# Turning x by halves into four banks, and a feature order that lets W_lat load in runs of 1024 bytes

## The reference

```
k = x @ W_lat + b_lat                        # (2, 512, 128), one for all heads; keys and values
q = x @ W_d + b_d                            # 16 heads of 128
att = softmax(causal(q k^T / sqrt(128)));  y = att @ k
x1 = layernorm(x + y @ W_proj + b_proj)
scores = x1 . router_weight + router_bias;   top 256 of 512 rows of each batch
rows picked: x1 += (gelu(x1 @ w1 + b1) @ w2 + b2) * sigmoid(score)
out = layernorm(x1)
```

## Time and profile before

| | us |
|---|---|
| median of 3 runs | 280.67 |
| lowest and highest | 280.57, 280.73 |
| the profiled execution | 280.85 |
| its span, first to last instruction | 279.1 |
| TensorE matmuls busy | 271.7 (97%) |
| VectorE, ScalarE, GpSimd busy | 218.8, 212.3, 154.2 |
| share of the 16 DMA engines taken by SyncE's queue | 16.4% |

### The profile page before, as it was taken

One profiled execution on the slowest core, in us unless ns is written; L12 is line 12 of the kernel. 1 busy time (PEld: TensorE's weight loads), 2 busy tenths in 40 slices (PEclk: granted clock), 3 DMA queues, 4 the chain that ended last, 5 costly groups with the idle time before them and its releaser, 6 DMA issues.

```text
span 279.1 us, 6206 instructions
## 1 busy us (share of the span) xinstructions
PE 271.7 (97%) x1885; PEld 247.0 (89%) x1885; DVE 218.8 (78%) x701; ACT 212.3 (76%) x578; POOL 154.2 (55%) x214
## 2 busy tenths in 40 slices
PE   8999999999999999999999999999999999999991
PEld 4878999999999998999999999999999999999990
DVE  2698777777777777788789888899988887779882
ACT  3689877777787778887787877787777778879471
POOL 5458444444433336555666866665657847238652
PEclk9999999999999999999999999999999999999997
DMA  5594110111101111111111111110112200020151
GB/s 178 144 293 124 39 40 28 30 36 38 34 25 35 38 39 38 40 38 42 38 38 40 38 40 38 39 37 22 38 39 79 78 21 21 1 76 2 58 171 38
DMA packets 18842, 15.53 MB, mean 56 GB/s; under 512 B 1641, under 2 KB 18178, under 8 KB 18818
## 3 DMA queue, kind: packets, MB, share of 16 engines
q1 hardware_dynamic: 18242, 13.65, 16.4%
q0 software_dynamic: 576, 1.58, 1.6%
HBM read 12.60 MB, written 2.63 MB: 55 GB/s over the span
## 4 chain that ended last, share of the span: by engine, by line
PE 97%; DVE 0%; POOLq 0%; issue 0%; ACT 0%; DVEq 0%
PE bank L412 21%; PE bank L414 20%; PE bank L413 20%; PE bank L547 9%; PE ps_out L412 7%; PE ps_out L413 6%; PE ps_out L414 6%; PE bank L527 3%; PE bank L637 3%; PE bank L470 1%; PE bank L424 1%; POOLq L60 0%; PE bank L676 0%; PE bank L678 0%; PE bank L557 0%
## 5 line engine op out<-in xcount | busy, mean ns | idle before, releaser
L841 ACT ACTIVATE probs<-probs,negmax 128x512 f32<-128x512 f32 (+3 forms) x128 | 72.6, 575 | 6.0 <-DVE negmax L1026 4.6
L1384 POOL TENSOR_TENSOR wd_hi<-wd_raw,zero 128x256 fp32r<-128x256 f32 x31 | 23.8, 768 | 87.5 <-DVE probs L1098 84.5
L849 ACT CAST pT_hi<-bank 128x512 fp32r<-128x512 f32 (+2 forms) x96 | 43.4, 488 | 27.7 <-PE bank L547 27.3
L1026 DVE CUSTOM_DVE_ANT_0 probs<-bank,mask_row 128x512 f32<-128x512 f32 (+3 forms) x128 | 59.2, 482 | 0.7 <-PE bank L504 0.7
L1035 DVE TENSOR_TENSOR pT_lo<-bank,pT_hi 128x512 fp32r<-128x512 f32 (+2 forms) x96 | 52.8, 552 | 6.0 <-ACT pT_hi L849 5.6
L547 PEld LDWEIGHTS bank<-ident_r,prob_words 128*128 128x128 f32 x310 | 33.0, 140 | 5.5 <-ACT probs L893 0.4
L412 PE MATMUL ps_out<-wp_hi,yT_hi 128*128 128x256 f32 x124 | 37.0, 299 | 0.0
L412 PE MATMUL bank<-kT_hi,qT_hi 128*128 128x256 f32 (+2 forms) x94 | 36.5, 388 | 0.0
L413 PE MATMUL ps_out<-wp_lo,yT_hi 128*128 128x256 f32 x124 | 35.0, 282 | 0.0
L414 PE MATMUL ps_out<-wp_hi,yT_lo 128*128 128x256 f32 x124 | 34.9, 282 | 0.0
L1055 DVE TENSOR_TENSOR yT_lo<-bank,yT_hi 128x512 fp32r<-128x512 f32 x31 | 21.4, 690 | 15.9 <-PE bank L414 14.1
(11 more groups left out here) (203 smaller groups left out, 732.1 us busy)
## 6 DMA issues: line engine op xcount, KB each, us to landing
wd_raw<-in_L_attn_W_d SPq DMA_DIRECT2D x32, 128.0 KB, 2.2
wp_raw<-in_L_attn_W_proj SPq DMA_DIRECT2D x32, 128.0 KB, 2.1
wf_raw<-in_L_ffn_w SPq DMA_DIRECT2D x2, 1024.0 KB, 6.7
x_nat<-in_L_attn_x SPq DMA_DIRECT2D x4, 256.0 KB, 3.4
out<-z_all SPq DMA_DIRECT2D x4, 256.0 KB, 2.3
picked<-ranked SPq DMA_DIRECT2D x2, 258.0 KB, 2.7
wlat_raw<-in_L_attn_W_lat SPq DMA_DIRECT2D x1, 128.0 KB, 3.8
bproj_all<-in_L_attn_b_proj SPq DMA_DIRECT2D x1, 128.0 KB, 3.4
```

What stands on the lines that cost most here:

```text
L841: act.activation(p_tile(s, j), p_tile(s, j), ACT.Exp, bias=negmax[:, s, j:j + 1], scale=-1.0, accum_out=sums[:, s, j:j + 1]).then_inc(exp_ ...
L849: act.copy(pT_hi[:, dst], src).then_inc(pt_hi_done, 1)
L1026: dve.tensor_tensor_reduce(p_tile(s, j), score_bank[j], mask_row[:, (TILES - 1 - j) * P:], -SCALE, -MASKED, ALU.add, ALU.min, accum_out=ne ...
L1384: pool.tensor_tensor(hi, src, nothing, ALU.add).then_inc(hi_done, 1)
```

## The change

- A chunk c holds the features c, c + 2, c + 4, ...: W_lat and W_d are loaded with the row 2 p + c on partition p, chunk c. So a partition's part of W_lat is two neighbouring rows, 1024 bytes in one run; of W_d a head's columns are still pieces of 512 bytes. The transposes of x read every second column of the rows as their stationary operand.
- The first batch's x is turned into four banks: half 0 into the first 256 columns of `ps_t0` and `ps_t1`, half 1 into those of `ps_s2` and `ps_s10`. ScalarE copies and VectorE subtracts each of the four by itself, 256 columns each; the semaphores count four steps for the first batch. The second batch is turned as before, apart from the columns read.
- An idle matmul of 256 columns stands between the two halves, and the two of 512 behind them become one of 512 and one of 256.
- VectorE does the two subtractions of half 0 ahead of the rounding of W_lat. The bias turning goes to `ps_s3`, and stands ahead of the last product for kT, whose terms are in another order.

```diff
+        x_banks = [[ps_t0[:, 0:KEEP], ps_t1[:, 0:KEEP]], [ps_s2[:, 0:KEEP], ps_s10[:, 0:KEEP]]]
+        def x_half(t, half, c):
+            return t[:, c, half * KEEP:(half + 1) * KEEP]
-        WAKING, AWAKE = 6, 2
+        WAKING, BETWEEN, AWAKE = 6, (2,), (4, 2)
-            wd = W_d.rearrange("(c p) n -> p c n", p=P)
+            wd = W_d.rearrange("(p c) n -> p c n", p=P)
-            sp.dma_start(wlat_raw[:], W_lat.rearrange("(c p) l -> p c l", p=P)).then_inc(wlat_in, 16)
+            sp.dma_start(wlat_raw[:], W_lat.rearrange("(p c) l -> p c l", p=P)).then_inc(wlat_in, 16)
                     for c in range(CH):
-                        dst = (ps_t0, ps_t1)[c]
+                        dst = (ps_t0, ps_t1)[c][:, half * KEEP:(half + 1) * KEEP] if b else x_banks[half][c]
                         if b and half == 0:
                             pe.wait_ge(x_split, c + 1)
-                        for j in range(2 * half, 2 * half + 2):
+                        for j in range(2):
                             last = pe.transpose(dst[:, j * P:(j + 1) * P].bitcast(F32R),
-                                                x_words[:, b * TILES + j, c * P:(c + 1) * P], ident_r[:, :])
-                        if half:
+                                                x_words[:, b * TILES + 2 * half + j, c:DIM:CH], ident_r[:, :])
+                        if half or not b:
                             last.then_inc(x_turned, 1)
+                    if not b and half == 0:
+                        keep_awake(BETWEEN)
 
             def project_k_first():
                 w_hi, w_lo, x_hi, x_lo = wlat_hi, wlat_lo, xT_hi[0], xT_lo[0]
+                def term(w, x, c, first=False, last=False):
+                    return pe.matmul(ps_kT, w[:, c, :], x[:, c, :], start=first, stop=last, skip_group_check=True)
                 pe.wait_ge(wlat_hi_done, 1)
-                pe.wait_ge(x_hi_done, 1)
-                pe.matmul(ps_kT, w_hi[:, 0, :], x_hi[:, 0, :], start=True, stop=False, skip_group_check=True)
-                pe.wait_ge(x_hi_done, 2)
-                pe.matmul(ps_kT, w_hi[:, 1, :], x_hi[:, 1, :], start=False, stop=False, skip_group_check=True)
-                pe.wait_ge(x_split, 1)
-                pe.matmul(ps_kT, w_hi[:, 0, :], x_lo[:, 0, :], start=False, stop=False, skip_group_check=True)
+                pe.wait_ge(x_hi_done, 3)
+                term(w_hi, x_hi, 0, first=True)
+                pe.wait_ge(x_hi_done, 4)
+                term(w_hi, x_hi, 1)
+                pe.wait_ge(x_split, 3)
+                term(w_hi, x_lo, 0)
                 pe.wait_ge(wlat_split, 1)
-                for c in range(CH):
-                    pe.matmul(ps_kT, w_lo[:, c, :], x_hi[:, c, :], start=False, stop=False, skip_group_check=True)
+                term(w_lo, x_hi, 0)
+                pe.wait_ge(x_split, 4)
+                term(w_hi, x_lo, 1)
                 pe.wait_ge(bias_in, 48)
-                pe.transpose(ps_s2[:, 0:BIASES], bias_rows[:, :], ident[0:BIASES, 0:BIASES]).then_inc(bias_turned, 1)
-                pe.wait_ge(x_split, CH)
-                pe.matmul(ps_kT, w_hi[:, 1, :], x_lo[:, 1, :], start=False, stop=True,
-                          skip_group_check=True).then_inc(kT_ready, 1)
+                pe.transpose(ps_s3[:, 0:BIASES], bias_rows[:, :], ident[0:BIASES, 0:BIASES]).then_inc(bias_turned, 1)
+                term(w_lo, x_hi, 1, last=True).then_inc(kT_ready, 1)
...
-            def keep_awake(times):
-                for _ in range(times):
-                    pe.matmul(ps_s3[:, :], still[:, :], still[:, :].unsqueeze(1).broadcast_to([P, TILES, P]),
+            def keep_awake(sizes):
+                for n in sizes:
+                    pe.matmul(ps_s3[:, 0:n * P], still[:, :], still[:, :].unsqueeze(1).broadcast_to([P, n, P]),
                               start=True, stop=True)
...
+            def x_high_halves():
+                for half in range(2):
+                    for c in range(CH):
+                        act.wait_ge(x_turned, CH * half + c + 1)
+                        act.copy(x_half(xT_hi[0], half, c), x_banks[half][c]).then_inc(x_hi_done, 1)
...
+            def x_low_half(half, c):
+                dve.wait_ge(x_hi_done, CH * half + c + 1)
+                dve.tensor_tensor(x_half(xT_lo[0], half, c), x_banks[half][c],
+                                  x_half(xT_hi[0], half, c).bitcast(F32), ALU.subtract).then_inc(x_split, 1)
...
+            x_low_half(0, 0)
+            x_low_half(0, 1)
             dve.wait_ge(wlat_in, 16)
             dve.tensor_copy(wlat_hi[:], wlat_raw[:]).then_inc(wlat_hi_done, 1)
             for c in range(CH):
-                x_low(0, c)
+                x_low_half(1, c)
             dve.wait_ge(bias_turned, 1)
-            dve.tensor_copy(bias_cols[:, :], ps_s2[:, 0:BIASES]).then_inc(bias_done, 1)
+            dve.tensor_copy(bias_cols[:, :], ps_s3[:, 0:BIASES]).then_inc(bias_done, 1)
```

More of the change, by code:

```diff
@@ L451, in project_k_second @@
                 for c in range(CH):
-                    pe.wait_ge(x_split, CH + c + 1)
+                    pe.wait_ge(x_split, 2 * CH + c + 1)
                     last = product(ps_kT, (wlat_hi[:, c, :], wlat_lo[:, c, :]),
@@ L464, in turn_k @@
                 last.then_inc(k_turned, 1)
-            def keep_awake(times):
-                for _ in range(times):
-                    pe.matmul(ps_s3[:, :], still[:, :], still[:, :].unsqueeze(1).broadcast_to([P, TILES, P]),
+            def keep_awake(sizes):
+                for n in sizes:
+                    pe.matmul(ps_s3[:, 0:n * P], still[:, :], still[:, :].unsqueeze(1).broadcast_to([P, n, P]),
                               start=True, stop=True)
             pe.wait_ge(still_filled, 1)
-            keep_awake(WAKING)
+            keep_awake((TILES,) * WAKING)
             pe.wait_ge(ident_r_done, 1)
@@ L542, in turn @@
                 if at.fixed == 1 and n < CH:
-                    pe.wait_ge(x_split, CH + n + 1)
+                    pe.wait_ge(x_split, 2 * CH + n + 1)
                 a = 0
@@ L798, in split_queries, with x_high_second @@
                                scale=1.0).then_inc(q_hi_done, 1)
-            def x_high(b):
+            def x_high_halves():
[3 more added lines that the diff above has]
+                        act.copy(x_half(xT_hi[0], half, c), x_banks[half][c]).then_inc(x_hi_done, 1)
+            def x_high_second():
                 for c in range(CH):
-                    act.wait_ge(x_turned, CH * b + c + 1)
-                    act.copy(xT_hi[b][:, c, :], (ps_t0, ps_t1)[c][:, :]).then_inc(x_hi_done, 1)
+                    act.wait_ge(x_turned, 2 * CH + c + 1)
+                    act.copy(xT_hi[1][:, c, :], (ps_t0, ps_t1)[c][:, :]).then_inc(x_hi_done, 1)
             def kT_high(b):
@@ L826, in k_high @@
                 act.copy(k_hi[b][:, :, :], ps_ks[b][:, 0:SEQ - P].rearrange("p (j l) -> p j l", l=LAT)).then_inc(k_hi_done, 1)
-            x_high(0)
+            x_high_halves()
             act.wait_ge(wd_in[0], 16)
@@ L834, in _ @@
             kT_bias(0)
-            x_high(1)
+            x_high_second()
             def exps(at, js):
@@ L988, in _, with x_low_second @@
             dve.memset(still[:, :], 0.0).then_inc(still_filled, 1)
[L990 to L993, removed]
+            def x_low_half(half, c):
+                dve.wait_ge(x_hi_done, CH * half + c + 1)
+                dve.tensor_tensor(x_half(xT_lo[0], half, c), x_banks[half][c],
+                                  x_half(xT_hi[0], half, c).bitcast(F32), ALU.subtract).then_inc(x_split, 1)
+            def x_low_second(c):
+                dve.wait_ge(x_hi_done, 2 * CH + c + 1)
+                dve.tensor_tensor(xT_lo[1][:, c, :], (ps_t0, ps_t1)[c][:, :],
+                                  xT_hi[1][:, c, :].bitcast(F32), ALU.subtract).then_inc(x_split, 1)
             def kT_low(b):
@@ L1069, in period @@
                     if at.fixed == 0:
-                        x_low(1, 0)
-                        x_low(1, 1)
+                        x_low_second(0)
+                        x_low_second(1)
                     wait(dve, scores_ready, p * 3 + 3)
```

## The result

The changed kernel takes 281.07 us (median of 22 runs, 280.89 to 281.49), the kernel before 280.65 in the same sessions (22 runs, 280.53 to 281.17). The ratio is 1.0014, with a 95% interval of 1.0009 to 1.0020: 0.4 us slower. The forecast was 0.2 faster. The profiled execution of the changed kernel took 281.09; its page reads as follows, beside the earlier trace rows: more span by 0.3, the same work of TensorE.

What follows compares the result with a forecast made beforehand. TensorE, busy 271.7 of 279.1 us, was taken to bound the kernel. Only the earlier kT start counted, 0.20 us, with strided reads and W_d at 0: 280.67 less 0.20 is 280.47 us, range 280.0 to 281.0.

Steps and rivals of the forecast that it cites:

- Copies, idle matmuls, VectorE's order, kT, first query: First 8 us: copies of x 4.31 to 5.76, idle matmuls to 5.72, rounding 5.40, first kT 5.76, query 2.01 later.
- the rival of a wait gone (280.1): Start: clock level rises before 5.76 (0.35) and bias turning shrinks by up to 0.2; 280.1 us, chance 0.13.
- Gain 0.20 us: Start of kT: first product at 5.76 instead of 5.96, 0.20 us earlier, carried over to the first scores.
- The load of W_lat: Start: 1024-byte pieces take 0.34 us instead of 0.54, so W_lat lands at 5.4 or sooner instead of 5.62.
- rival 1: The start does not move: W_lat lands as before or the clock level rises as late as 6.40; 280.67 us, chance 0.15.
- Reading every second column. I take 0: Transposes of x: sixteen weight loads stepping over 8 bytes cost 0, like the nearest contiguous loads; upper end twice as long.
- The bounds of 0 and 0.4: Later eight strided transposes: no cost at the lower end; at half rate 0.4 us, after 0.15 hides behind qT_hi.
- rival 2: Transposes of x: strided weight loads at half rate, 0.13 more each early, 0.07 late, 0.85 together; 281.5 us, chance 0.10.
- Nothing there has a time of its own, and a shift at 10 us should still stand at the end: After 20 us: TensorE's weight-side waits are 0.2 us at most and for ScalarE, so the 0.20 gained early stays.
- the chances for shifts in the later periods: Later periods: shifts that the profile rows don't price, chance 0.10 for faster by over 0.2%, 0.04 for slower.

Runs made afterwards that it cites:

- b2: Changed kernel with contiguous transposes and old weight layout, plus two more instructions each on ScalarE and VectorE: 280.68 against 280.67 for the kernel before (1.0001).
- b1: Kernel before with two more instructions each on ScalarE and VectorE, placed ahead of the loop without moving the table load: 280.92 against 280.67 (1.0012).
- b4: Changed kernel with two more instructions each on ScalarE and VectorE: 280.70 against 280.67 for the kernel before (1.0006).
- c1: Kernel before, unchanged, run again for a second profile: 280.64 against 280.71 (0.9991).
- a3: Kernel before with strided transposes and the new layout of both weights, no halves: 280.70 against 280.68 (0.9996).
- a2: Changed kernel with contiguous transposes and the old weight layout, halves kept: 280.98 against 280.68 for the kernel before (1.0004).

## Why the prediction was wrong, step by step

- **Copies, idle matmuls, VectorE's order, kT, first query: right.** 4.27 and 5.66 (forecast 4.31 and 5.76), 5.43, 5.77, 1.99 us on. Where the biases are turned made no difference, the rival of a wait gone (280.1) did not appear, and the first query did not wait for W_d.
- **"Gain 0.20 us": a term mis-sized.** The sum set a forecast start against one profiled execution, in which W_lat was late. Against the other executions of the kernel before the halves start no earlier: first products at 5.96, 5.72, 5.63, 5.52, 5.91, 5.70 and 5.77 with the old start, 5.77, 5.66, 5.60, 5.79, 5.86 and 5.80 with the new; first scores, read contiguously, between 9.86 and 10.39 (five traces) with the old, 9.96, 9.98 and 10.10 with halves. b2 against the kernel before is 0.01 us, with an interval of 0.3 to 0.4 to either side. I put the gain at 0 to 0.1, an estimate.
- **The load of W_lat: no difference.** From issue to landing it took 3.6, 3.4, 3.4 and 3.5 us with 1024-byte pieces, and 3.3 to 3.8 in the eleven traces with 512 in which SyncE issues it. By the rates of the earlier trace rows the transfer is 0.34 or 0.54 of these 3.3 to 3.8 us, and the 0.2 between the two do not show in them; rival 1 said so, and has its part of the outcome (280.67 was its time).
- **"Reading every second column. I take 0": a term mis-sized.** 0.12 us at the first scores. The bounds of 0 and 0.4 held it; I had taken the lower end for being the nearest shape. Each of the late weight loads starts 0.14 behind the last instead of 0.09, an extra 0.055, near the 0.07 of rival 2. The eight take 0.41 more; rival 2 let 0.15 hide behind qT_hi, and 0.29 of it did. The early eight cost 0.01 to 0.02 each, not 0.13. The Trainium skill's note on 16-byte lines in SBUF (SBUF — State Buffer, "Door 1: The DMA port swizzle (why [64,N] ≈ [32,N])"), by which four fp32 can be stepped over for free, does not agree with these weight loads.
- **"Nothing there has a time of its own, and a shift at 10 us should still stand at the end": the step that failed.** There are delays behind 10 us that belong to places in the engines' instruction streams, and the change put other instructions on these places. The two late instructions cost 0.29 to 0.30 in the trace, +0.25 in the median of b1; b4 is 0.37 below the changed kernel, though measured in another session. No term and no rival priced what two more instructions per engine do to the rest of the program. Only the chances for shifts in the later periods, 0.10 for faster and 0.04 for slower, stood for it.

Together: 0.3 for the two late instructions, 0.1 for the stride, 0 to 0.1 off for the start, against 0.4 measured. The prediction's range (280.0 to 281.0) ended 0.07 short.

What is shown: the steps come with the count, each with its own engine's. VectorE's late instruction is the 408th with two more and with six more, ScalarE's the 64th with two more and with four more; where the steps are gone, a wait or a long operation stands over the place. A transfer of instructions goes with each place. Not shown is why passing it costs about 0.3 us: the transfer seen there starts behind the late instruction, so it is not what that one waits for. The Trainium skill (Runtime: NRT & Kernel Launch, "Instruction fetch mechanics") says that the sequencer streams instructions in blocks of 256, and that crossing into one is mostly hidden. The traces agree in part: the kernel before has the same transfers and no step. But the pieces here are of 8192 bytes, and "mostly hidden" is 0.3 to 0.4 us when it is not. What the engine does in these 0.3 us stays open.

## What to carry to other kernels

When a small change adds instructions on an engine, expect the rest of the program to shift in its instruction stream, and before blaming the change, run the kernel before with as many idle instructions, and the new one with a few more. If the time then comes back, the delay may still be there, covered: look for it in the trace before calling it gone. A wait that a profile shows for a DMA is one draw: a gain that rests on it needs a second execution, or a range that allows for no gain. And a bound is not settled by the nearest shape: the new access cost 0.12 us of the 0.4 that its range had.

## What the hardware did that I had not expected

- A late instruction in the middle of a stream: ScalarE's yT_hi 0.3 us late, VectorE's pT_lo 0.36 late, in every trace with two instructions more on that engine, to 0.01 us.
- The table load of ScalarE goes behind waits that stand ahead of the first activation: 4.93 instead of 0.8 us, and the kernel took 2.9 us more.
- Weight loads with a stride of two fp32 start 0.14 us apart at either level of the clock; contiguous ones 0.09 at the higher and 0.127 at the lower.
- The moment of the change from 1.2 to 2.4 GHz differs between executions of one program: the first two products for kT stand 0.59 us apart in one execution of the kernel before (c1) and 0.44 in another; b1, with the same start, has 0.34. The first scores of kernels with the old start and contiguous reads lie anywhere from 9.86 to 10.39; a3, with strided reads and 0.62 between its first two products, has them at 10.64.
- Issuing W_d's load as pairs of rows costs SyncE half as much again, though pieces and bytes are the same (min, median, max ns over 32 issues). Changed kernel, then before; a3, with the layout alone, has 548 as the median, a2, without it, 368; nothing waited for it:

```profile
L353 SPq DMA_DIRECT2D wd_raw<-in_L_attn_W_d x32: 540/547/663, 2.3 to 207.9; - x32
```

```profile
L348 SPq DMA_DIRECT2D wd_raw<-in_L_attn_W_d x32: 367/368/469, 2.3 to 207.7; - x32
```
